# An adapter feed-forward kernel whose adapters are loaded whole and picked on chip, with the expert flips spread over fewer chunks

## The reference

```python
# x (8, 512, 2048) f32, one adapter index per batch: itok_B (8,), values 3..7
# cond:  Bx  = einsum('bni,bri->bnr', x, B[itok])          # B (8 adapters, 16, 2048)
#        y   = einsum('bnr,bor->bno', Bx, A[itok])         # A (8 adapters, 2048, 16)
# ffn:   base_out   = einsum('bsi,oi->bso', y, base_w) + base_b      # base_w (2048, 2048)
#        res_hidden = einsum('bsi,ri->bsr', y, ffn_A)                # ffn_A (64, 2048)
#        probs      = softmax(einsum('bsi,ei->bse', y, router_w))    # 16 experts
#        topw, topi = top_k(probs, 2); topw = topw / (sum(topw) + 1e-6)
#        combine    = sum over k of one_hot(topi) * topw
#        delta      = einsum('bse,bsr,eor->bso', combine, res_hidden, ffn_B)  # ffn_B (16, 2048, 64)
# out = x + base_out + 0.5 * delta
```

## Time and profile before

| | |
|---|---|
| median of 3 runs | 500.61 us (500.36 to 502.29) |
| the profiled execution | 499.74 us, span of its trace 497.9 us |
| PE busy | 414.2 us (83%) |
| DVE busy | 285.9 us (57%) |
| ACT busy | 124.3 us (25%) |
| POOL busy | 45.0 us (9%) |
| moved by DMA | 135.30 MB, 272 GB/s on average |

### The profile page before, as it was taken

How to read it: one execution, slowest core, us unless ns; L and a number is a source line. 1 busy time by engine, 2 the same in 40 slices (tenths; PEclk the granted TensorE clock), 3 DMA queues, 4 the chain that set the end, 5 groups by cost and what they waited for, 6 DMA issues and landing times.

```text
span 497.9 us, 5920 instructions
## 1 busy us (share of the span) xinstructions
PE 414.2 (83%) x2112; PEld 249.2 (50%) x2112; DVE 285.9 (57%) x627; ACT 124.3 (25%) x170; POOL 45.0 (9%) x46
## 2 busy tenths in 40 slices
PE   0000699797787899999999999999999999999997
PEld 0000365243343456655655675565566566556675
DVE  1301158845273575677767567676666756776443
ACT  1000237437276102301310230220131023013210
POOL 3510000000012001200120120020012012001200
PEclk9999999989798899999999999999999999999999
DMA  8759986979789679999999999999999999935854
GB/s 289 165 128 310 328 227 171 306 215 280 240 297 291 226 196 288 334 339 265 266 371 288 278 339 336 269 327 363 241 285 372 307 280 327 352 111 181 309 201 169
DMA packets 93780, 135.30 MB, mean 272 GB/s; under 512 B 14068, under 2 KB 46836, under 8 KB 93748
## 3 DMA queue, kind: packets, MB, share of 16 engines
q1 hardware_dynamic: 67764, 108.69, 71.2%
q10 hardware_dynamic: 25986, 26.22, 20.4%
HBM read 99.24 MB, written 35.65 MB: 271 GB/s over the span
## 4 chain that ended last, share of the span: by engine, by line
PE 66%; DMA 15%; DVE 10%; issue 3%; SPq 3%; ACT 1%; ACTq 1%; DVEq 0%
PE ps L754 11%; PE ps L771 11%; DMA early_u<-in_L_ffn_B 10%; PE ps L772 9%; PE ps L773 9%; PE ps L718 7%; PE ps L785 6%; PE ps L774 5%; PE ps L708 3%; DVE xT L593 3%; DVE h_r L583 3%; DMA tok<-in_itok_B 3%; DVE xbuf L696 2%; DMA g_hilo<-u_r 2%; PE ps L796 2%
## 5 line engine op out<-in xcount | busy, mean ns | idle before, releaser
L696 DVE TENSOR_TENSOR xbuf<-ps,xbuf 128x512 f32<-128x512 f32 x128 | 86.8, 678 | 105.2 <-PE ps L774 104.9
L771 PE MATMUL ps<-h_r,u_r 128*128 128x512 f32 x256 | 109.2, 427 | 9.5 <-DVE xbuf L696 9.5
L772 PE MATMUL ps<-h_r,u_r 128*128 128x512 f32 x256 | 100.3, 392 | 0.0
L773 PE MATMUL ps<-h_r,u_r 128*128 128x512 f32 x256 | 100.1, 391 | 0.0
L708 PE MATMUL ps<-ident,early_u 128*128 128x128 f32 x128 | 26.3, 289 | 65.5 <-DMA early_u<-in_L_ffn_B 65.5
L771 PEld LDWEIGHTS ps<-h_r,u_r 128*128 128x128 f32 x256 | 48.0, 188 | 51.2 <-issue 20.3
L718 PE MATMUL ps<-early 128*128 128x512 f32 x128 | 70.9, 638 | 1.5 <-DVE early L544 1.4
L593 DVE STREAM_TRANSPOSE xT<-xbuf 128x512 f32<-128x512 f32 x112 | 72.0, 680 | 0.0
L708 PEld LDWEIGHTS ps<-ident,early_u 128*128 128x128 f32 x128 | 18.4, 149 | 100.9 <-issue 88.4
L754 PE MATMUL ps<-bexpT,cur 128*32 128x512 f32 x512 | 64.3, 622 | 3.7 <-ACT bexpT L407 3.7
L544 DVE STREAM_TRANSPOSE early<-xbuf 128x512 f32<-128x512 f32 x64 | 43.3, 691 | 38.2 <-PE ps L718 38.1
(11 more groups left out here) (62 smaller groups left out, 209.1 us busy)
## 6 DMA issues: line engine op xcount, KB each, us to landing
xbuf<-in_x SPq DMA_DIRECT2D x32, 1024.0 KB, 7.9
out<-xbuf SPq DMA_DIRECT2D x31, 1024.0 KB, 7.2
xbuf<-in_x SPq DMA_DIRECT2D x28, 512.0 KB, 11.2
xbuf<-in_x ACTq DMA_DIRECT2D x28, 512.0 KB, 9.5
xbuf<-in_L_ffn_base_w SPq DMA_DIRECT2D x8, 1024.0 KB, 14.0
xbuf<-in_L_ffn_base_w ACTq DMA_DIRECT2D x8, 1024.0 KB, 11.8
early_u<-in_L_ffn_B SPq DMA_DIRECT2D x16, 512.0 KB, 10.8
gm_r<-g_hilo SPq DMA_DIRECT2D x128, 32.0 KB, 6.5
```

Source lines behind the costliest of these rows:

```text
L696: dve.tensor_tensor(xs, ps[:, ACC + t % 2, :], xs, ALU.add).then_inc(s_out, 1)
L771: pe.matmul(acc, u_r[:, b.q, 0, h, tok_t], hi, start=(h == 0), stop=False)
L772: pe.matmul(acc, u_r[:, b.q, 0, h, tok_t], lo, start=False, stop=False)
L773: pe.matmul(acc, u_r[:, b.q, 1, h, tok_t], hi, start=False, stop=False)
```

## The change

Seven edits, all in the front:

1. A and B of all 8 adapters are loaded, from fixed addresses: A by 32 transfers (16 from SP, 16 from ACT, 32 KB each as before), B by four of 256 KB from ACT. Nothing waits for the indices any more before loading. The bytes are the same, since there are as many adapters as batches.
2. The choice is made on chip. ACT makes `a_t` by 8 copies (128x256) whose source address is a register, in place of 4 copies (128x512). DVE transposes B of all adapters into a part of `xT`, and POOL picks from it by 8 copies into `bT`. For that ACT and POOL read 8 indices each from SBUF into registers.
3. The order of loads: on SP, expert 0 now stands ahead of base_w group 1, and the bias and router_w behind experts 1 and 2. On ACT, ffn_A follows base_w group 1, and ACT's table load and the reading of indices stand behind all the loads.
4. PE flips 9 pieces per 4 chunks (`FLIPS`), not 8: expert e is done in chunks 3, 7, 10, 14, 17, 21, 24, 28, 31, 35, 39, 42, 46, 49, 53 and 56, in place of 3, 7, 11, ... 63. SP loads expert 11 ahead of group 3, and experts 12 to 15 ahead of x's first block.
5. `ga_products` follow chunk 12 (before 3), `sel_products` chunk 15 (before 8), with DVE's parts at 14 and 18; DVE transposes B at chunk 9 (before 3) and ffn_A at chunk 11 (before: ahead of the loop).
6. The first `h_products` of batch 0 stand behind chunk 60 (before: behind the loop).
7. The first of the two copies of an expert walks its elements in the other order, so that it writes in steps of 8 bytes, as the second does, and no longer in steps of 64.

```diff
-        GA_AFTER, SEL_AFTER = 3, 8
-        BT_AT, GA_AT, SEL_AT = 3, 6, 11
+        GA_AFTER, SEL_AFTER = 12, 15
+        BT_AT, FA_AT, GA_AT, SEL_AT = 9, 11, 14, 18
+        H_AFTER = 60
+        FLIPS = [min(EF * E, 9 * (n + 1) // 4) for n in range(NW)]
...
+        def expert_done(n):
+            return [e for e in range(E) if (FLIPS[n - 1] if n else 0) < EF * (e + 1) <= FLIPS[n]]
...
-        def load_adapters(eng, half):
...
+        def load_cond_a(eng, ns):
+            for n in ns:
                 for q in range(NQ):
+                    eng.dma_start(conda_q[q * SQ:(q + 1) * SQ, n, :, :], condA_q[n, q]).then_inc(s_conda, 16)
...
             load_w(sp, 0, (0, 1))
+            load_cond_a(sp, range(0, NAD // 2))
+            load_expert(0)
+            load_w(sp, 1, (0, 1))
+            for e in range(1, 3):
+                load_expert(e)
...
-            sp.wait_ge(s_tok, 16)
-            load_adapters(sp, 1)
-            load_w(sp, 1, (0, 1))
-            for e in range(3):
-                load_expert(e)
             for u in range(2):
                 load_xquad(sp, 0, u, (0, 1), xquad0)
...
-            for e in range(8, 11):
+            for e in range(8, 12):
                 load_expert(e)
             sp.wait_ge(s_wt, 2 * KD)
             load_w(sp, 3, (0, 1))
-            load_expert(11)
+            load_expert(12)
             store_g(1)
...
+            pool.wait_ge(s_tok, 16)
+            ids = [adapter(pool, b) for b in range(NB)]
+            pool.wait_ge(s_bT, KC)
+            pool.wait_ge(s_biaslo, 1)
+            for b in range(NB):
+                pool.tensor_copy(bT[:, :, b // 2, b % 2 * RK:(b % 2 + 1) * RK],
+                                 bT_all[:, :, bass.ds(ids[b], 1), :].rearrange("p j n k -> p j (n k)"))\
+                    .then_inc(s_bsel, 1)
...
+            act.dma_start(tok[:, :], itok.rearrange("(a b) -> a b", a=1)).then_inc(s_tok, 16)
             load_w(act, 0, (2, 3))
+            load_cond_a(act, range(NAD // 2, NAD))
+            for q in range(NQ):
+                act.dma_start(condb_q[q * SQ:(q + 1) * SQ], condb_v[q]).then_inc(s_condb, 16)
+            load_w(act, 1, (2, 3))
+            for q in range(NQ):
+                act.dma_start(ffna_q[q * SQ:(q + 1) * SQ, 0:R // SQ, :], ffna_v[q]).then_inc(s_small, 16)
+            for u in range(2):
+                load_xquad(act, 0, u, (2, 3), xquad0)
...
             act.wait_ge(s_tok, 16)
+            ids = [adapter(act, b) for b in range(NB)]
+            act.wait_ge(s_conda, 16 * NAD * NQ)
+            for b in range(NB):
+                copy(a_t[:, :, b * RK:(b + 1) * RK].rearrange("p (a r) k -> p a r k", r=2),
+                     conda_q[:, bass.ds(ids[b], 1), :, :].rearrange("p n a (r k) -> p (n a) r k", r=2)).then_inc(s_a, 1)
...
-                copy(dst[:, 0], src[0:R])
-                copy(dst[:, 1].rearrange("r h m -> r m h"), src[R:P].rearrange("r h m -> r m h"))\
-                    .then_inc(s_ec, 1)
+                for l in range(2):
+                    ins = copy(dst[:, l].rearrange("r h m -> r m h"), src[l * R:(l + 1) * R].rearrange("r h m -> r m h"))
+                ins.then_inc(s_ec, 1)
...
+                for k in range(FLIPS[n - 1] if n else 0, FLIPS[n]):
+                    expert_flip(k)
                 w_product(n)
...
-            pe.wait_ge(s_ec, E)
-            h_products(first, 0)
+                if n == H_AFTER:
+                    pe.wait_ge(s_ec, E)
+                    h_products(first, 0)
             pe.wait_ge(s_glo, W_GROUPS)
```

More of the change, by code:

```diff
@@ L53, in adaln_ffn @@
     MT = OC * NT
-    assert T == BANK and NB * RK == P and 2 * R == P and EH * RK == P and D == O
+    assert T == BANK and NB * RK == P and NAD * RK == P and 2 * R == P and EH * RK == P and D == O
     W_GROUPS = O // (NT * P)
@@ L229, in xquad_free, with adapter @@
             eng.wait_ge(s_xe, f.n * KD + (g + 1) * KD // 2)
-        def load_adapters(eng, half):
-            ids = {}
-            for b in range(half, NB, 2):
-                ids[b] = eng.value_load(tok[0:1, b:b + 1], min_val=0, max_val=NAD - 1)
+        def load_cond_a(eng, ns):
+            for n in ns:
                 for q in range(NQ):
[L237 to L243, removed]
+                    eng.dma_start(conda_q[q * SQ:(q + 1) * SQ, n, :, :], condA_q[n, q]).then_inc(s_conda, 16)
+        def adapter(eng, b):
+            return eng.value_load(tok[0:1, b:b + 1], min_val=0, max_val=NAD - 1)
         block = ctx.enter_context(nc.Block())
@@ L297, in _ @@
             load_w(sp, 3, (0, 1))
-            load_expert(11)
+            load_expert(12)
             store_g(1)
-            for e in range(12, 15):
+            for e in range(13, 16):
                 load_expert(e)
@@ L413, in _ @@
             act.wait_ge(s_tok, 16)
[L414 to L421, removed]
+            ids = [adapter(act, b) for b in range(NB)]
[3 more added lines that the diff above has]
+                     conda_q[:, bass.ds(ids[b], 1), :, :].rearrange("p n a (r k) -> p (n a) r k", r=2)).then_inc(s_a, 1)
             def copy_expert(e):
                 act.wait_ge(s_ef, e + 1)
-                for pair, there, count in ((0, s_a, KC), (1, s_bT, KC), (2, s_fat, 2), (3, s_sm, 1), (4, s_xe, KD)):
+                for pair, there, count in ((0, s_a, NB), (1, s_bT, KC), (2, s_fat, 2), (3, s_sm, 1), (4, s_xe, KD)):
                     if e == 2 * pair:
@@ L491, in _ @@
                         load_xquad(act, 1, u, (2, 3))
-                if n % 4 == 3:
-                    copy_expert(n // 4)
+                for e in expert_done(n):
+                    copy_expert(e)
                 if n in SLOT_AT:
@@ L527, in _, with ffna_transposes @@
                                 pick[:, q, :].unsqueeze(1).to_broadcast([P, P // RK, RK])).then_inc(s_masks, 1)
[L529 to L533, removed]
+            def ffna_transposes():
+                dve.wait_ge(s_small, 2 * NQ * 16)
+                by_r = ffna_q.rearrange("p t (a l r) -> p r a t l", l=SQ, r=2)
+                to_r = ffnaT.rearrange("p (a r) (t l) -> p r a t l", r=2, l=SQ)
+                for r in range(2):
+                    dve.transpose(to_r[:, r], by_r[:, r]).then_inc(s_fat, 1)
             def w_transpose(n):
@@ L665, in _ @@
                     b_transposes()
+                if n == FA_AT:
+                    ffna_transposes()
                 if n == GA_AT:
@@ L719, in w_product, with expert_flip @@
                           stop=(s == KD - 1)).then_inc(s_wmm, 1)
-            def expert_flips(e, hs):
-                if hs[0] == 0:
+            def expert_flip(f):
+                e, h = f // EF, f % EF
+                if h == 0:
                     pe.wait_ge(s_ein[e % 3], 16 * (e // 3 + 1))
                     need(pe, s_ec, e - 1)
-                for h in hs:
-                    ins = flip(e_bank(e) + h // 4, h % 4 * P, e_in[e % 3][:, h * P:(h + 1) * P])
-                if hs[-1] == EF - 1:
+                ins = flip(e_bank(e) + h // 4, h % 4 * P, e_in[e % 3][:, h * P:(h + 1) * P])
+                if h == EF - 1:
                     ins.then_inc(s_ef, 1)
@@ L733, in ga_products @@
                 pe.wait_ge(s_fat, 2)
-                pe.wait_ge(s_a, KC)
                 for s in range(KD):
```

33 lines of the change are left out of this document (17 added, 16 removed).

## The result

| | before | after |
|---|---|---|
| median | 500.49 us (499.83 to 502.29, 4 runs) | 510.26 us (505.66 to 511.77, 4 runs) |
| ratio, 95% interval | | 1.0174 [1.0103, 1.0245] |
| the profiled execution | 499.74 us, span 497.9 | 510.71 us, span 508.8 |
| ACT busy | 124.3 us | 111.9 us |

The kernel is 1.7% slower, and the interval of the ratio lies wholly above 1. The forecast of 501.1 us was wrong, and the time lies outside its range of 495.5 to 506. It went the way of the slower rival, and farther than its 505.5.

The account below looks back on a forecast made before the run. PE is busy from 174 us on, so the front's DMA gaps and waits bound the start. Last store 0.85 us earlier, clock +1.4: +0.5 on 499.74, 500.3; median 0.87 above, 501.1 us; 8-in-10 range 495.5 to 506.

Parts of the forecast that it names:

- the slower rival: At ACT's loads ahead of a_t: late loads delay the first product, 505.5 us in all; chance 0.26.
- Gate 1: PE's first product: predicted at 51.6 us, 3.5 earlier than before; bounds 7.0 earlier and 5.2 later.
- The condition: At ACT's x loads: its queue takes the last one when only the four x loads are left in it.
- 7.34 MB at 315 GB/s, to 44.0: ACT's B, group 1 and ffn_A plus as much for SP's queue: 23.3 us, ending ACT's x issue at 44.0.
- late bound: Slow end of each term before the first product; all together put it at 60.3 us, 5.2 later than before.
- ACT's queue holds its copies: ACT's loads stand ahead of a_t; decides from x issue ending at 46.0; half of 8.7 us, 505.5; chance 0.26.
- Gates 2 to 5: Group 2 issued 74.3; expert 7 landed 95.15, group 3 issued 104.15; next expert landed 126.8; last store landed 169.45 us.
- The wait for expert 7: PE ahead of chunk 25, before in chunk 28: a wait of 4 to 5 us.
- The price of the clock: PE idle over 5 us after batch 0's third tile, then at a lower clock: 1.4 us lost, bounds 0 and 2.

Follow-up runs that it names:

- e3: The changed kernel with the index load moved behind ACT's half of base_w group 0: 504.05 us, ratio 1.008 to the kernel before.
- e7: e3 with group 0 dealt in turns, SP loading partitions 0 to 31 and 64 to 95, ACT the others: 509.63 us, one run.
- e2: The changed kernel with two flips per chunk, first h_products behind the last chunk and SP's earlier order of experts 11 to 15: 506.08 us.
- e6: The changed kernel with indices behind group 0, ACT's copies behind its group 1, experts 1 and 2 ahead of SP's group 1, x loads spread out: 487.21 us.
- e8: The changed kernel with the first h_products put back behind chunk 63: 509.41 us, ratio 1.0151 to the kernel before.
- e9: The kernel before, with ACT's copies into a_t moved ahead of its four x loads: 501.35 us, ratio 1.0029.
- e4: The changed kernel with the first copy of an expert writing in steps of 64 bytes again: 508.5 us, ratio 1.0186 to the kernel before.
- e1: The changed kernel with ACT's index readings and copies into a_t ahead of its ffn_A and x loads: 500.31 us, ratio 0.9987 to the kernel before.
- e5: As e6, but with two flips per chunk, the earlier order of experts 11 to 15 and first h_products behind the last chunk: 485.84 us, ratio 0.9661.
- e10: e5 with the four ffn_A transfers ahead of ACT's half of base_w group 1: 483.3 us, ratio 0.9686 to the kernel before.

## Why the prediction was wrong, step by step

- **Gate 1 failed, by 9.7 us.** The condition was right: the queue takes the last x load when the loads ahead of the four are through. ACT's loads ahead of them (its halves of group 0, A and group 1, then B and ffn_A) are 6.29 MB, and its queue had moved 6.38 MB by 53.85. The term "7.34 MB at 315 GB/s, to 44.0" was wrong in both of its numbers. The A transfers were issued at 22.46, 1.8 us after the 20.7 at which I had them through. From there to 53.85, in 31.39 us, the two queues moved 8.59 MB at 274 GB/s. I had given SP's queue as much as ACT's, 3.67 MB; it moved 4.71. At 315 GB/s the further 1.25 MB are 4.0 us, and all 8.59 MB at 274 instead of 315 are 4.1 more: 1.8 + 4.0 + 4.1 = 9.9, the 9.85 by which the end of the issue was off. Behind it the readings took 4.66 and not 4.4, and the copies 2.67 and not 3.2, so the first product was off by 9.7.
- **The low rate has a cause that I did not look for, and perhaps a second.** I took group 0 at 346 GB/s though the diff puts a transfer ahead of it; it ran at 281. e3 gives that edit 4.2 us of the 9.7. And from 26.4 to 33.6 us the changed kernel moved only 215 GB/s, near e7's 212. By the order of the queues SP was then at its first quarters of group 1 and ACT at its first quarters of B, both in partitions 0 to 63. At 315 GB/s these 7.2 us would be 4.9, an estimate of 2.3 us. That the partitions are the reason there is argued from e7; no run tries it.
- **The second failure: what counts as a late bound.** The late ends summed to 60.3, and the first product came at 61.27. Each end was a rate taken from the kernel before, where other things stood in the queues. The rival "ACT's queue holds its copies" had the mechanism and the point from which it decides (46.0); I priced it at half of its late bound.
- **Gates 2 to 5 held as distances, in part by luck.** From gate to gate: group 2 23.2 us after the first product (22.7 predicted), expert 7 19.7 after that (20.85), group 3 8.9 later (9.0), the next expert 23.4 later (22.6), the x loads 27.5 later (26.4), the store 16.0 after them (16.3). The errors of about 1 us cancel: from first product to store it was 118.6, predicted 117.85. The wait for expert 7 is ahead of chunk 25, as forecast, and in this trace the 3.5 us are given back there; e2 and e6 point the same way, inside their noise. That expert 7 is issued at chunk 17 in both kernels was misread: before, it went out behind chunk 19, at 83.55, but 4.3 us behind group 2, where it is 4.5 now, so nothing hung on it.
- **The price of the clock came true, but not for the reason given.** PE's granted clock after the last wait was 0.50, the 1.2 GHz level, and the rest of the span took 1.3 us more (1.4 predicted). I put that down to edit 6. But e8, without edit 6, has 0.50 there too and a rest of 327.5 us. The kernel of e9, which has none of the seven edits, idled only 2.50 us there, fell to 0.50 as well and has 326.1. The kernel before idled 1.77 us and kept 1.00, and its rest is 325.0. So the amount is partly luck.
- **Edits 6 and 7 are worth nothing that can be measured here.** e8 and e4. An expert's copies take 1.10 us each; the 12 us of ACT's time saved lie beside waits.
- **Where the gain of the first three edits went.** The wait of 13.90 us in the earlier trace rows did go, and expert 0 was there by 26.9 instead of 54.68. None of it reached the first product. The first product needs expert 0 and the copies: e9 brought the copies alone and gained nothing, the change brought expert 0 alone and lost, e1 brought both and then waited for experts 2 and 3, and e5 brought those sooner too.

## What to carry to other kernels

An engine that issues transfers and also computes can be held in the issue, as ACT was here for 17.30 us: put its short work ahead of the last big loads, and price such a block with all bytes that the other queue can move in that time. Removing a wait at the head of a chain pays only as far as the second latest arrival; list all arrivals that the first product and the next few steps need before giving the gain a number. With the other edits kept and only the order of transfers and copies mended, e6 took 4.7% off the changed kernel (0.9699/1.0174), more than any one edit here cost or gave.

## What the runs showed of the hardware

- Two queues that fill the same 64 partitions first share a rate of 212 GB/s (e7, one run), against 320 to 346 with one half each (before, e3, e5, e6, e9, e10).
- A transfer of 32 bytes ahead of ACT's first 2 MB brought the first 12 us from 330 down to 281 GB/s (e3 against the changed kernel): over 2 to 8 us ACT's queue moved 0.18 MB instead of 0.84.
- Issuing four x loads of 512 KB took ACT 13.58 to 17.96 us and SP 16.95 to 21.53 us when megabytes stood ahead in the queue, and 2.36 us when none did (163.90 in the changed kernel).
- After PE had idled 2.50 to 7.26 us ahead of the tiles its granted clock was 0.50 to 0.59 for the next 3 us in all eleven traces that have such a wait; after 1.77 us (before) it stayed at 1.00.
